# First layer norm's rows made by ScalarE instead of GpSimd, in a new cyclic order of four engines

## The chip, the core and the metric

The kernel runs on one core of one Trainium2 chip. A core has four compute engines that run their own instruction streams: TensorE (PE, matmuls and transposes), VectorE (DVE), ScalarE (ACT) and GpSimd (POOL). SyncE (SP) issues DMAs. They meet only through semaphores. The metric is the device time of the whole program in microseconds; lower is better.

## The reference

Two layers over x of 64 sequences, 128 tokens, 256 features. The phase that matters here is the first layer's attention and its router:

```python
x = x + _L0_xattn_ref(_layernorm(x), ctx_768, mask, Wq, Wk, Wv, Wo)   # 16 heads of 16, softmax over 128 keys
x = x + _L0_ffn_ref(_layernorm(x), w_switch, b_switch, w1, b1, w2, b2) # 8 experts, capacity 512
x = x + _L1_xattn_ref(_layernorm(x), ctx_768, ...)
x = x + _L1_ffn_ref(_layernorm(x), ew, act_w, We, be, Wq, Wk, Wv, Wo, ln_g, ln_b)

def _layernorm(x, axis=-1, eps=1e-05):
    m = jnp.mean(x, axis=axis, keepdims=True)
    v = jnp.var(x, axis=axis, keepdims=True)
    return (x - m) / jnp.sqrt(v + eps)
```

The router picks an expert for each token and counts, over all tokens before it, how many went to the same expert; that count is the token's slot.

## The kernel before, in words

The program has three phases: the first layer's attention with routing (`phase_first_layer`, to about 650 us), the experts (`phase_experts`), and the second layer (`phase_second_layer`), which takes most of the time. The change is in the first.

The phase handles 64 sequences in 32 jobs of two. The steps of a job have short names, and each engine walks through its own list of (step, job) pairs:

- `st` (VectorE): `bn_stats` and `bn_aggr` of the job's x, into mean and variance; `rs` (GpSimd): 1/sqrt(variance + eps), two small operations; `nm`: the normalized rows `xn`, made by GpSimd with a `tensor_scalar` for each sequence (subtract mean, multiply by rstd).
- `Tx`, `K`, `Q`, `V` (TensorE): transpose of `xn`, and the projections. A name with `^` is the VectorE step that empties the product's PSUM bank, such as `Tx^` into `xT`, `Q^`, `K^` (two operations, even and odd heads), `V^`.
- `S0`, `S1` (TensorE): the scores of sequence 0 or 1 for 16 heads in four PSUM banks, one for each strip of four heads. A bf16 mask row is written first (L645), then the products (L654). `S0.x2` (VectorE) is the row maximum of strip 2 (L488), `S0.e2` (ScalarE) its exponentials, four activations with row sums (L432), `S0.i2` (VectorE) the reciprocals of the sums (L491), `S0.n2` (GpSimd) the product that normalizes the probabilities (L384).
- `T0.0`, `T0.1`, `T1.0`, `T1.1` (TensorE): transposes of the probabilities of two strips each (L664), copied out of PSUM by ScalarE (`T0^0` and so on, L438).
- `A`, `O` (TensorE) with `A^`, `O^`: attention output, output projection; `O^` adds x. `st1`, `rs1`, `nm1`: the second layer norm, on VectorE and GpSimd, into a ring `xn1`. `Tn`, `L`: its transpose and the router's logits.
- `r.sh`, `r.ex`, `r.oh`, `r.n`, `r.n^`: the routing of a group of jobs (groups end at jobs 3, 7, ..., 27, 29, 31). `r.oh` (VectorE, L560 to L569) is a chain of 16 small operations that wait for each other. `put` (GpSimd): two indirect DMAs a job that scatter `xn1` into the experts' buffer.

All products but the scores share four PSUM banks in the order in which TensorE writes them: a product waits until the one four before it has been emptied.

The order is cyclic and written out. In `FIRST_PE_ORDER` the entry `A:3` says that in round k the step `A` of job k - 3 runs. `unfold` turns a table into the whole list; `FIRST_PE_TAIL` and `FIRST_DVE_TAIL` put the last jobs' steps at the end in an order of their own, together with the first six fused weights (`F`, `B`) of the second layer. An engine stands still at a step whose inputs are missing, with everything behind it.

SyncE's list: load of x for job j (waits for `nm1` of job j - 4, whose slot in a ring of four it takes), load of the context, store of x1 and of xn1 of job j - 3, and so on.

Of the kernel before, what the change touches and what calls it, by code (L numbers as in the profile page):

```python
# [11 lines left out]
ALU = mybir.AluOpType  # L12
# [4 lines left out]
PAIR = 2  # L17
# [101 lines left out]


FIRST_PE_ORDER = """
K:1 T0.1:3 S1:2 Tx:1 A:3 r.n:6 Q:1 O:3 T1.0:2 T0.0:2 S0:1 V:1 L:5 Tn:4 T1.1:2
"""

FIRST_DVE_ORDER = """
r.oh:5 S0.i0:1 K^:0 S0.i1:1 S1.x0:1 Tx^:0 S1.x1:1 S1.x3:1 S1.i0:1 A^:2 r.n^:5 S1.x2:1 S1.i1:1 Q^:0 S1.i3:1
O^:2 S0.i3:1 S1.i2:1 st1:2 S0.i2:1 S0.x0:0 S0.x1:0 S0.x3:0 V^:0 L^:4 r.sh:4 mk:-1 st:-1 S0.x2:0 Tn^:3
"""

FIRST_ACT_ORDER = """  # L130
S1.e1:1 S1.e3:1 S1.e2:1 T1^0:1 T1^1:1 T0^0:1 T0^1:1 S0.e0:0 S0.e1:0 S0.e3:0 r.ex:4 T1^2:1 S0.e2:0 T1^3:1
T0^3:1 T0^2:1 S1.e0:0
"""

FIRST_POOL_ORDER = """
rs:1 nm:1 rs1:4 S0.n0:2 nm1:4 S0.n1:2 S1.n0:2 S1.n1:2 S1.n3:2 S1.n2:2 S0.n3:2 S0.n2:2 put:9
"""


# [13 lines left out]
def phase_first_layer(nc, io, scratch, keep, cst, consts_in, cell, first):  # L153
# [7 lines left out]
    CAP = int(CAP_FACTOR * B * T / E)  # L161
    JOBS = B // PAIR
    W2 = PAIR * T
    X_RING, ROW_RING, GROUP = 4, 6, 4
    MASK_JOBS, SENDS, RING = 4, 3, 3
    plan = cell_plan()
    fused = fused_weights(plan)
# [52 lines left out]
    with ExitStack() as es:  # L220
# [3 lines left out]
        def sem(name):  # L224
# [8 lines left out]
        one_row = sb("one_row", [P], BF16)  # L233
        stats, mv = sb("stats", [2, PAIR, 6]), sb("mean_var", [2, 2, PAIR, 2])
        veps, rstd = sb("var_eps", [2, 2, PAIR]), sb("rstd", [2, 2, PAIR])
        qT = sb("qT", [2, 2, W2])
        kE, kO = first["kT_even"], sb("kT_odd", [2, 2, W2])
        va = sb("v_even_odd", [2, PAIR, PAIRS_OF_HEADS, 4, 16])
# [31 lines left out]
        stat, var_made, veps_made, rstd_made = \  # L270
            ([sem(f"{n}{i}") for i in range(2)] for n in ("stats_made", "var_made", "veps_made", "rstd_made"))
        zero_made, buf_zeroed = sem("zero_made"), sem("buf_zeroed")
        step, shifted, exped, hot, slots_made = \
            sem("vector_step"), sem("shifted"), sem("exped"), sem("one_hot"), sem("slots_made")

# [83 lines left out]
        def _(pool):  # L359
# [18 lines left out]
            for n, j in on_pool:  # L378
# [6 lines left out]
                                            ALU.mult).then_inc(norm_made, 1)  # L385
                elif n == "rs":
                    rsqrt(0, j)
                elif n == "rs1":
                    rsqrt(1, j)
                elif n == "nm":  # L390
                    if j >= 1:
                        pool.wait_ge(prod, n_prod["Tx", j - 1])
                    normal(xt[:, j % X_RING], xn, 0, j, xn_made)
                elif n == "nm1":
                    if j >= ROW_RING:
                        p = j - ROW_RING
# [21 lines left out]
        def _(act):  # L418
# [7 lines left out]
            for n, j in on_act:  # L426
                if is_round(n):

                    b, r = head_strip(n)
                    act.wait_ge(max_made, n_max[f"S{b}.x{r}", j])  # L430
                    for k in range(4):
                        a = nc.scalar.activation(pr[:, j % 2, b, r, k], S[r][:, k], ACT.Exp, bias=nmax[:, j % 2, b, r, k:k + 1],  # L432
                                                 accum_out=rsum[:, j % 2, b, r, k:k + 1])
                    a.then_inc(exp_made, 1)
                elif is_turn(n):

                    act.wait_ge(turned, n_turn[n, j])
                    nc.scalar.copy(pT[:, int(n[1]), int(n[-1])], bank(n, j)[:]).then_inc(pT_made, 1)  # L438
                elif n == "r.ex":
                    act.wait_ge(shifted, group_at[j] + 1)  # L440
                    t0, t1 = tiles_of[group_at[j]]
                    nc.scalar.activation(e[:, 0:t1 - t0], pb[:, 0:t1 - t0], ACT.Exp).then_inc(exped, 1)
                else:
                    raise ValueError(n)

        @block.vector
        def _(dve):
# [8 lines left out]
            def statistics(src, i, j):  # L456
# [6 lines left out]
                    dve.wait_ge((xn_made, xn1_made)[i], j - 1)  # L463
                for b in range(PAIR):
                    k = V.bn_aggr(mv[:, i, j % 2, b], stats[:, i, b])
                k.then_inc(var_made[i], 1)

            def chain(i):
# [1170 lines left out]
```

## Time and profile before

| | us |
|---|---|
| median of three runs (4090.85 to 4096.52) | 4091.06 |
| the profiled execution's own time | 4089.82 |
| its span | 4088.0 |
| TensorE busy | 4001.1 (98%) |
| ScalarE busy | 2622.6 (64%) |
| VectorE busy | 2392.3 (59%) |
| GpSimd busy | 1930.2 (47%) |

```profile
## 2 busy tenths in 40 slices
PE   8999999999999999999999999999999999999997
PEld 6888886668888888888888888888888888888886
DVE  5777772025566656666666666666665666666553
ACT  6888881215666666666666666666666666666664
POOL 5888883113444444444444444444444444444443
PEclk9999999999999999999999999999999999999999
```

A slice is 102 us, a digit tenths of it. The first phase is the first six slices: there four engines are at seven to nine tenths at once. Busy time on TensorE includes time in which a matmul waits in its pipeline, so it is not a bound by itself. PEclk is the granted clock as a share of 2.4 GHz.

### The profile page before, as it was taken

How to read it: one execution, taken by the hardware profiler on the slowest of the kernel's cores; microseconds unless marked ns; L12 is line 12 of the kernel's file. 1: busy time of each engine (PE TensorE's matmuls, PEld its weight loads, DVE VectorE, ACT ScalarE, POOL GpSimd, SP SyncE). 2: the span in 40 equal slices, each digit the busy share in tenths (PEclk: the TensorE clock that was granted, in tenths of full speed). 3: DMA queues.
4: the chain of work that ended last, by engine and by line, in shares of the span. 5: the costliest groups of instructions: out<-in, count | busy, mean ns of one | idle time of the engine just before them, and what ended most of it. 6: DMA issues, size and time to landing. Idle time of an engine off the chain costs nothing.

```text
span 4088.0 us, 100757 instructions
## 1 busy us (share of the span) xinstructions
PE 4001.1 (98%) x38276; PEld 3410.6 (83%) x38276; DVE 2392.3 (59%) x6184; ACT 2622.6 (64%) x11786; POOL 1930.2 (47%) x2011
## 2 busy tenths in 40 slices
PE   8999999999999999999999999999999999999997
PEld 6888886668888888888888888888888888888886
DVE  5777772025566656666666666666665666666553
ACT  6888881215666666666666666666666666666664
POOL 5888883113444444444444444444444444444443
PEclk9999999999999999999999999999999999999999
DMA  3232214521000000000000000000000000000000
GB/s 104 70 97 70 67 53 138 181 73 35 14 13 16 15 14 14 13 14 17 14 13 13 14 13 13 20 12 12 12 12 12 12 12 12 12 12 12 7 4 9
DMA packets 117866, 129.73 MB, mean 32 GB/s; under 512 B 12006, under 2 KB 110676, under 8 KB 117264
## 3 DMA queue, kind: packets, MB, share of 16 engines
q1 hardware_dynamic: 105648, 109.80, 8.4%
q0 software_dynamic: 6144, 8.43, 0.7%
q8 instruction: 311, 5.10, 0.5%
q10 hardware_dynamic: 5600, 5.07, 0.4%
q14 instruction: 163, 1.34, 0.1%
HBM read 89.68 MB, written 41.94 MB: 32 GB/s over the span
## 4 chain that ended last, share of the span: by engine, by line
PE 76%; DVE 1%; ACT 0%; issue 0%; POOL 0%; POOLq 0%; ACTq 0%
PE c_product L1411 37%; PE c_product L1422 15%; PE c_product L1470 11%; PE c_scores L1460 7%; PE c_product L1493 5%; PE c_product L1481 2%; DVE c_qT L1266 1%; PE c_product L1399 1%; ACT c_probs L1223 0%; PE c_product L1530 0%; ACT c_front_probs L1223 0%; DVE c_nodes L1266 0%; DVE c_neg_max L1275 0%; POOL c_probs L1177 0%; DVE c_nodes L1337 0%
## 5 line engine op out<-in xcount | busy, mean ns | idle before, releaser
L1177 POOL TENSOR_TENSOR c_probs<-c_probs,c_row_inv 128x512 f32<-128x512 f32 x768 | 794.9, 1043 | 1390.4 <-DVE c_row_inv L1278 1384.4
L1223 ACT ACTIVATE c_probs<-c_scores,c_neg_max 128x128 f32<-128x128 f32 x3072 | 1084.3, 407 | 354.0 <-DVE c_neg_max L1275 353.9
L1411 PE MATMUL c_product<-c_nodes,cell_w 128*128 128x256 f32 x4352 | 1067.4, 384 | 4.8 <-DVE c_nodes L1266 3.1
L1411 PEld LDWEIGHTS c_product<-c_nodes,cell_w 128*128 128x128 f32 x4352 | 797.4, 190 | 123.7 <-DVE c_nodes L1266 11.8
L1223 ACT ACTIVATION_READ_ACCUMULATOR c_probs<-c_scores,c_neg_max 128x1 f32 x3072 | 759.3, 247 | 0.0
L1275 DVE TENSOR_REDUCE c_neg_max<-c_scores 128x4 f32<-128x512 f32 x1024 | 658.3, 679 | 169.5 <-PE c_scores L1460 161.7
L1229 ACT COPY c_probsT<-c_product 128x512 f32<-128x512 f32 x768 | 419.8, 600 | 462.2 <-PE c_product L1470 458.2
L1223 ACT ACTIVATE c_front_probs<-c_scores,c_neg_max 128x128 f32<-128x128 f32 x1024 | 364.7, 394 | 170.2 <-DVE c_neg_max L1275 170.2
L1422 PE MATMUL c_product<-cell_w,c_nodes 128*128 128x256 f32 x1792 | 430.3, 381 | 0.0
L432 ACT ACTIVATE a_probs<-a_scores,a_neg_max 128x128 f32<-128x128 f32 x1024 | 361.2, 399 | 83.9 <-DVE a_neg_max L488 83.2
L1470 PE MATMUL c_product<-consts_sb,c_probs 128*128 128x128 f32 x3072 | 404.1, 275 | 5.4 <-POOL c_probs L1177 5.4
L1470 PEld LDWEIGHTS c_product<-consts_sb,c_probs 128*128 128x128 f32 x3072 | 355.4, 141 | 46.6 <-POOL c_probs L1177 7.3
L1177 POOL TENSOR_TENSOR c_front_probs<-c_front_probs,c_row_inv 128x512 f32<-128x512 f32 x256 | 270.0, 1056 | 258.4 <-DVE c_row_inv L1278 256.8
L1422 PEld LDWEIGHTS c_product<-cell_w,c_nodes 128*128 128x128 f32 x1792 | 329.4, 191 | 38.6 <-issue 0.6
L1278 DVE RECIPROCAL c_row_inv<-c_row_sum 128x4 f32<-128x4 f32 x1024 | 167.9, 169 | 329.2 <-ACT c_probs L1223 225.4
L1411 PE MATMUL c_product<-c_oT,cell_w 128*128 128x256 f32 x1280 | 329.3, 380 | 0.0
L384 POOL TENSOR_TENSOR a_probs<-a_probs,a_row_inv 128x512 f32<-128x512 f32 x256 | 258.9, 1041 | 28.6 <-DVE a_row_inv L491 28.5
L1411 PEld LDWEIGHTS c_product<-c_oT,cell_w 128*128 128x128 f32 x1280 | 243.1, 190 | 34.5 <-DVE c_oT L1266 2.3
L1266 DVE TENSOR_SCALAR c_oT<-c_product,cell_b 128x256 f32<-128x256 f32 x384 | 167.8, 478 | 140.0 <-PE c_product L1493 139.1
L1266 DVE TENSOR_SCALAR c_qT<-c_product,cell_b 128x256 f32<-128x256 f32 x384 | 166.3, 474 | 136.4 <-PE c_product L1411 134.8
L432 ACT ACTIVATION_READ_ACCUMULATOR a_probs<-a_scores,a_neg_max 128x1 f32 x1024 | 245.1, 239 | 0.0
L1223 ACT ACTIVATION_READ_ACCUMULATOR c_front_probs<-c_scores,c_neg_max 128x1 f32 x1024 | 238.8, 233 | 0.0
(167 smaller groups left out, 6450.2 us busy)
## 6 DMA issues: line engine op xcount, KB each, us to landing
e_w<-in_L_ffn_w SPq DMA_DIRECT2D x12, 1024.0 KB, 6.2
a_x<-in_x SPq DMA_DIRECT2D x32, 256.0 KB, 2.9
a_ctxT<-in_ctx_pairsT SPq DMA_DIRECT2D x32, 256.0 KB, 3.1
x<-a_x SPq DMA_DIRECT2D x32, 256.0 KB, 2.1
xn<-a_xn SPq DMA_DIRECT2D x32, 256.0 KB, 2.2
c_routed<-xn SPq DMA_DIRECT2D x32, 256.0 KB, 2.7
c_x<-x SPq DMA_DIRECT2D x32, 256.0 KB, 3.1
c_ctxT<-in_ctx_pairsT SPq DMA_DIRECT2D x32, 256.0 KB, 2.8
```

The costliest lines, as they stand in the source:

```text
L384: nc.gpsimd.tensor_tensor(p, p, rinv[:, j % 2, b, r].unsqueeze(2).broadcast_to([P, 4, T]), ALU.mult).then_inc(norm_made, 1)
L432: a = nc.scalar.activation(pr[:, j % 2, b, r, k], S[r][:, k], ACT.Exp, bias=nmax[:, j % 2, b, r, k:k + 1], accum_out=rsum[:, j % 2, b, r, ...
L1177: nc.gpsimd.tensor_tensor(e, e, rinv[:, i, r].unsqueeze(2).broadcast_to([P, 4, T]), ALU.mult).then_inc(norm_made, 1)
L1223: a = nc.scalar.activation(probs(n)[:, r, k], S[r][:, k], ACT.Exp, bias=nmax[:, i, r, k:k + 1], accum_out=rsum[:, i, r, k:k + 1])
L1229: nc.scalar.copy(probsT(n)[:, int(n[-1])], bank(n, j)[:]).then_inc(pT_made, 1)
L1266: k = V.tensor_scalar(dst[:, u], m[:, u], bias[:, u:u + 1], scalar, ALU.add, *([then] if then else []))
L1275: V.tensor_reduce(nmax[:, i, r], S[r][:], AX.X, ALU.max, negate=True).then_inc(max_made, 1)
L1411: i = T_.matmul(m[:, u], w[:, k, u * P:(u + 1) * P], src[:, k], start=n == 0, stop=n == last)
L1422: i = T_.matmul(m[:, b], src[:, k, b * T:(b + 1) * T], w[:, k], start=n == 0, stop=n == len(steps) - 1)
L1460: i = T_.matmul(S[r][:, k], q[e, u, b * T:(b + 1) * T], w[e, u, b * T:(b + 1) * T], start=True, stop=True)
L1470: i = T_.transpose(m[:, k], probs(name)[:, r, k], ident)
L1493: i = T_.matmul(m[32 * r:32 * r + 32, u, b * T:(b + 1) * T], va[:, group(c), b, h:h + 32], pT[:, group(c), r, k], start=True, stop=True)
```

## The change

The normalized rows of the first layer norm are made by ScalarE, as Identity(rstd * x + shift) with shift = -mean * rstd. VectorE writes the negated mean in `st`, GpSimd multiplies it by rstd in `rs`. The four cyclic tables are replaced; the ring of `xn1` grows from 6 to 8 jobs. The tail tables stay.

```diff
 FIRST_PE_ORDER = """
-K:1 T0.1:3 S1:2 Tx:1 A:3 r.n:6 Q:1 O:3 T1.0:2 T0.0:2 S0:1 V:1 L:5 Tn:4 T1.1:2
+Tn:6 Q:1 T0.1:3 T1.1:3 S0:1 A:3 r.n:7 K:0 O:3 T1.0:2 T0.0:2 S1:1 L:6 Tx:0 V:1
 """
 
 FIRST_DVE_ORDER = """
-r.oh:5 S0.i0:1 K^:0 S0.i1:1 S1.x0:1 Tx^:0 S1.x1:1 S1.x3:1 S1.i0:1 A^:2 r.n^:5 S1.x2:1 S1.i1:1 Q^:0 S1.i3:1
-O^:2 S0.i3:1 S1.i2:1 st1:2 S0.i2:1 S0.x0:0 S0.x1:0 S0.x3:0 V^:0 L^:4 r.sh:4 mk:-1 st:-1 S0.x2:0 Tn^:3
+O^:3 S1.i3:2 st1:3 S0.i1:1 S0.i3:1 S0.i0:1 S0.i2:1 S1.x3:1 S1.x2:1 S1.x1:1 Tx^:0 L^:6 S1.x0:1 r.sh:6 V^:1
+Tn^:5 Q^:0 r.oh:6 S1.i1:1 S1.i0:1 st:-1 S0.x2:0 S0.x0:0 S0.x3:0 A^:2 r.n^:6 S1.i2:1 S0.x1:0 mk:-2 K^:-1
 """
 
 FIRST_ACT_ORDER = """
-S1.e1:1 S1.e3:1 S1.e2:1 T1^0:1 T1^1:1 T0^0:1 T0^1:1 S0.e0:0 S0.e1:0 S0.e3:0 r.ex:4 T1^2:1 S0.e2:0 T1^3:1
-T0^3:1 T0^2:1 S1.e0:0
+nm:-1 T0^1:1 S1.e3:0 S1.e2:0 S1.e1:0 r.ex:5 S1.e0:0 T0^3:1 T0^2:1 T1^3:1 T1^2:1 S0.e2:-1 S0.e3:-1 S0.e0:-1
+S0.e1:-1 T1^0:0 T1^1:0 T0^0:0
 """
 
 FIRST_POOL_ORDER = """
-rs:1 nm:1 rs1:4 S0.n0:2 nm1:4 S0.n1:2 S1.n0:2 S1.n1:2 S1.n3:2 S1.n2:2 S0.n3:2 S0.n2:2 put:9
+S0.n3:2 nm1:4 put:11 S0.n1:2 S1.n0:2 rs:0 S0.n2:2 S1.n1:2 S0.n0:2 S1.n2:2 S1.n3:2 rs1:3
 """
...
-    X_RING, ROW_RING, GROUP = 4, 6, 4
+    X_RING, ROW_RING, GROUP = 4, 8, 4
...
                 elif n == "rs":
                     rsqrt(0, j)
+                    pool.wait_ge(rstd_made[0], j + 1)
+                    nc.gpsimd.tensor_tensor(shift[:, j % 2], neg_mean[:, j % 2], rstd[:, 0, j % 2], ALU.mult).then_inc(shift_made, 1)
                 elif n == "rs1":
                     rsqrt(1, j)
-                elif n == "nm":
-                    if j >= 1:
-                        pool.wait_ge(prod, n_prod["Tx", j - 1])
-                    normal(xt[:, j % X_RING], xn, 0, j, xn_made)
...
+                elif n == "nm":
+
+                    act.wait_ge(shift_made, j + 1)
+                    if j >= 1:
+                        act.wait_ge(prod, n_prod["Tx", j - 1])
+                    for b in range(PAIR):
+                        k = nc.scalar.activation(xn[:, b], xt[:, j % X_RING, b], ACT.Identity, bias=shift[:, j % 2, b:b + 1],
+                                                 scale=rstd[:, 0, j % 2, b:b + 1])
+                    k.then_inc(xn_made, 1)
...
                 for b in range(PAIR):
                     k = V.bn_aggr(mv[:, i, j % 2, b], stats[:, i, b])
+                if i == 0:
+                    k.then_inc(mean_made, 1)
+                    dve.wait_ge(mean_made, j + 1)
+                    k = V.tensor_scalar(neg_mean[:, j % 2], mv[:, 0, j % 2, :, 0], -1.0, None, ALU.mult)
                 k.then_inc(var_made[i], 1)
```

## Rows read from the trace of the kernel before

**Rows 1.** Timeline of VectorE: `Tx^`; columns start us, duration us, instruction.

```profile
438.45 0.69 DVE L500 COPY a_xT<-a_product 128x512 f32<-128x512 f32 x1
...
459.30 0.68 DVE L500 COPY a_xT<-a_product 128x512 f32<-128x512 f32 x1
...
478.30 0.69 DVE L500 COPY a_xT<-a_product 128x512 f32<-128x512 f32 x1
...
496.09 0.69 DVE L500 COPY a_xT<-a_product 128x512 f32<-128x512 f32 x1
```

**Rows 2.** Timeline of VectorE: first maxima of `S1`, jobs 1 and 31.

```profile
50.34 0.69 DVE L488 TENSOR_REDUCE a_neg_max<-a_scores 128x4 f32<-128x512 f32 x1 [2.19 <-PE a_scores L654]
...
607.20 1.89 DVE L488 TENSOR_REDUCE a_neg_max<-a_scores 128x4 f32<-128x512 f32 x3
```

**Rows 3.** Groups by line, GpSimd, 263.5 to 281.3 us: count, busy us, mean ns, idle.

```profile
L384 POOL TENSOR_TENSOR a_probs<-a_probs,a_row_inv 128x512 f32<-128x512 f32 x8 | 8.1, 1041 | 0.0
L370 POOL TENSOR_SCALAR a_xn<-a_x,a_mean_var,a_rstd 128x256 f32<-128x256 f32 x4 | 4.9, 1220 | 0.2 <-POOL a_rstd L365 0.2
L411 POOL DMA_INDIRECT buf<-a_xn,slots x2 | 2.1, 1041 | 0.5 <-issue 0.5
L365 POOL TENSOR_TENSOR a_rstd<-a_var_eps,consts_sb 128x2 f32<-128x2 f32 x2 | 1.4, 716 | 0.2
L363 POOL TENSOR_TENSOR a_var_eps<-a_mean_var,consts_sb 128x2 f32<-128x2 f32 x2 | 0.4, 186 | 0.3 <-DVE a_mean_var L465 0.3
```

**Rows 4.** Timeline of TensorE: transposes of probabilities, and mask rows of scores.

```profile
218.77 0.60 PE L664 MATMUL a_product<-consts_sb,a_probs 128*128 128x128 f32 x4
219.59 1.53 PE L664 MATMUL a_product<-consts_sb,a_probs 128*128 128x128 f32 x12 [0.22 <-POOL a_probs L384]
221.05 0.40 PE L645 MATMUL a_scores<-a_mask_add,a_one_row 32*128 32x512 bf16 x4
...
241.30 1.91 PE L664 MATMUL a_product<-consts_sb,a_probs 128*128 128x128 f32 x16
243.14 0.40 PE L645 MATMUL a_scores<-a_mask_add,a_one_row 32*128 32x512 bf16 x4
...
251.04 0.76 PE L645 MATMUL a_scores<-a_mask_add,a_one_row 32*128 32x512 bf16 x4
```

**Rows 5.** Busy us of each engine in stretches of 20 us, then clock, DMA, GB/s.

```profile
220.00:240.00 20.00, 17.32 (x209) 14.86 (x208) 16.52 (x56) 13.89 (x65) 15.36 (x18) 0.91 0.49 154
...
480.00:500.00 20.00, 19.78 (x234) 17.09 (x227) 14.75 (x40) 17.67 (x87) 18.91 (x21) 1.00 0.20 61
```

**Rows 6.** Timelines of TensorE and VectorE in one routing round.

```profile
233.76 3.60 PE L675 MATMUL a_product<-a_probsT,a_v_even_odd 128*32 128x128 f32 x64 [1.78 <-DVE a_kT_odd L506]
...
228.62 0.21 DVE L560 TENSOR_REDUCE a_mx<-a_exp 128x8 f32<-128x64 f32 x1
...
232.33 0.72 DVE L505 TENSOR_SCALAR front_keys<-a_product,consts_sb 128x512 f32<-128x512 f32 x1
```

**Rows 7.** Groups by line and shape, ScalarE, whole program.

```profile
L432 ACT ACTIVATE a_probs<-a_scores,a_neg_max 128x128 f32<-128x128 f32 x1024 | 361.2, 399 | 83.9 <-DVE a_neg_max L488 83.2
...
L438 ACT COPY a_probsT<-a_product 128x512 f32<-128x512 f32 x256 | 141.1, 635 | 15.7 <-PE a_product L664 15.5
...
L432 ACT ACT_TABLE_LOAD x1 | 1.3, 1283 | 24.0 <-DVE a_neg_max L488 24.0
```

**Rows 8.** SyncE's timeline at a load of x, and the loads' median to landing.

```profile
575.13 0.40 SPq L298 DMA_DIRECT2D a_x<-in_x  x1
...
a_x<-in_x SPq DMA_DIRECT2D x28, 256.0 KB, 2.8
```

**Rows 9.** Timelines of GpSimd and TensorE at the phase's end.

```profile
629.16 2.43 POOL L370 TENSOR_SCALAR a_xn<-a_x,a_mean_var,a_rstd 128x256 f32<-128x256 f32 x2 [0.21 <-POOL a_rstd L365]
...
646.57 0.97 POOL L411 DMA_INDIRECT buf<-a_xn,slots  x1 [0.30 <-issue]
...
653.16 1.57 PE L831 MATMUL e_turned<-consts_sb,front_keys 128*128 128x128 f32 x8 [1.35 <-DMA front_keys<-buf]
```

More of the change, by code:

```diff
@@ L235, in phase_first_layer @@
         veps, rstd = sb("var_eps", [2, 2, PAIR]), sb("rstd", [2, 2, PAIR])
+        neg_mean, shift = sb("neg_mean", [2, PAIR]), sb("shift", [2, PAIR])
         qT = sb("qT", [2, 2, W2])
@@ L272, in phase_first_layer @@
         zero_made, buf_zeroed = sem("zero_made"), sem("buf_zeroed")
+        mean_made, shift_made = sem("mean_made"), sem("shift_made")
         step, shifted, exped, hot, slots_made = \
```

## The prediction

> **What bounds the kernel now.** The table of engines comes first: TensorE is busy for 98% of the span, and the change touches only the first of three phases, which ends with the first expert matmul near 653 us. A busy TensorE looks like a bound, so the second view is the beat of the phase. The copy `Tx^` runs once a job: its starts stand 17.79 us apart in plain jobs, and 20.85 and 19.00 us apart in the two around a routing group [rows 1]. Between the score maxima of job 1 and those of job 31 lie 556.86 us [rows 2]; 30 beats of 17.79 are 533.7, so the routing groups, of which seven fall in or at the edge of this stretch, cost 23.2 us, 3.3 each.
>
> Third, GpSimd over one beat (17.8 us): 8.1 for the probabilities' products, 4.9 for both layer norms, 2.1 for the indirect DMAs, 1.4 and 0.4 for the small steps and 0.9 of gaps, together 17.8 [rows 3]. It never rests: GpSimd sets the plain beat, and TensorE's busy share hides that. Fourth, what TensorE loses in such a beat. Sixteen transposes take 1.84 us from start to start where nothing is waited for (241.30 to 243.14), and 2.28 where the last twelve wait for GpSimd's product (218.77 to 221.05); the mask rows of a round of scores take 0.40 us unhindered (243.14), and 0.76 where they wait for exponentials (251.04) [rows 4]. Without these two losses of 0.44 and 0.36 the beat would be 16.99 us: TensorE's floor.
>
> Fifth, the routing stall. `r.oh` holds VectorE from 228.62 to 232.25, `K^` comes only behind it at 232.33, and the matmuls of `A`, which need the bank that `K^` empties, start after 1.78 us of idling and last 3.60 us instead of 1.9, because the granted clock has fallen from 2.4 to 1.2 GHz (mean 0.91 in this stretch) [rows 5, 6].
>
> **The change, part by part.**
> Taken off GpSimd: two TENSOR_SCALAR of 1.22 us a job [rows 3], 2.4 us. Added: one product of 2 columns, nearest to L363's 0.19 us [rows 3], and a wait for rstd of about 0.2. GpSimd then needs 17.8 - 2.4 + 0.4 = 15.8 us with its waits. It stops being the bound.
>
> Added on ScalarE: two Identity activations of 256 columns with scale and bias. None is in the trace. Below: two Exp of 128 columns, 0.40 us each; above: two copies of 512 columns, 0.64 us each [rows 7]. So 0.8 to 1.3 us for the pair; 1.0 taken, between both. In a plain stretch ScalarE is busy for 17.67 of 20 us [rows 5], 15.7 of a beat; with the pair 16.7, which is 0.3 under TensorE's floor. At the upper bound it is the floor itself.
> The Trainium skill, ScalarE: Activation LUTs, section What ACT_TABLE_LOAD costs, speaks against this price: an ACTIVATE with one pointer operand takes 280 ns and 0.833 ns a column, a second pointer adds 93 ns. An estimate by it is 1.08 us for the pair, and a ScalarE sum of 16.8 us; the forecast would not move. No row here shows that form.
>
> Added on VectorE: a 2-column negation after the aggregates, 0.17 us like the reciprocals, and a wait of some 0.1 us for its own result. VectorE is busy for 14.75 of 20 us [rows 5], 13.1 of a beat; 13.4 does not bind.
>
> **The new order.** It adds no matmul. I laid its cycle out with TensorE at its floor (time 0 is the start of `Tn:6`; `S0` starts at 4.1, `A` 5.4, `K` 7.3, `O` 9.0, `T1.0` 10.7, `S1` 12.6, `Tx` 14.6, `V` 15.1) and looked for links that come too late. `A` needs the four pT copies of ScalarE just in time; `O` needs `A^` with 1 us to spare; the bank of `T0.0` needs `K^` with 1.1; that of the second `T0.0` strip needs `O^` with 0.65; `Tx` needs ScalarE's `nm` with 0.5, and `nm` needs GpSimd's shift with 6. `S0` and `S1` find their score banks emptied 1 us before. The tightest ring runs through the load of x: `nm1` ends, SyncE issues the store and then the load (0.4 us an issue), it lands 2.8 us later [rows 8], and `st` must follow before VectorE's `S0.x2`; about 0.8 us is left. All fit at 16.99, with half a microsecond in several places, so I take **17.2** as the beat: 16.99 and 0.2 for waits that the layout leaves out.
>
> In the routing round `r.oh` now stands ahead of `S0.x2`, `A^` and `K^`, and it still costs 3.6 us. `A^` comes 1.0 us too late for `O`, `K^` 0.5 more for `T0.0`, `O^` 0.2 more, and r.n's own matmuls are 0.5: 2.2 us instead of 3.3. Idle pieces of 1.0 and 0.5 us instead of 1.78 should mostly spare the fall of the clock. Bounds: 0.5 (its work alone) and 4.3 (the 3.06 and 1.21 of [rows 1]).
>
> The sum: 30 x 17.2 + 6 x 2.2 = 529.2 against 556.86, **-27.7 us** (the seventh group falls in the drain).
>
> **Fill.** `S1` of job 0 now needs no full round of its own: `S0`, `K`, `S1` stand in one round. The table load (1.28 us [rows 7]) moves ahead of the first `nm`, where it delays the first transposes by 0.3 us, and leaves the first Exp. By my layout job 1's maxima come 3 us earlier (bounds -5 and +1).
>
> **Drain.** Here the deeper order takes back. Before, `nm1` of the last job ends at 631.59, 24.4 us after the landmark at 607.20; then six `put` follow, 12 indirect DMAs to 647.54, so 2.54 us a `put` without the one wait of 0.7; the experts start at 653.16 [rows 2, 9]. After, `put:11` leaves eight of them behind that `nm1` (20.3 us), and `nm1` itself ends some 26.7 us after the landmark, because `S1.n3` and `O` of the last job come later. 26.7 + 20.3 + 5.6 = 52.6 instead of 46.0: **+6.6 us**. TensorE has run out of fused-weight work by then and may start the experts at 1.2 GHz: +1.
>
> Total -27.7 - 3 + 6.6 + 1 = -23.1 us. The profiled execution took 4089.82 us, 1.2 below the median of the three runs, so 4066.7 for it and **4068 us** on the median's footing. What stands behind the first phase runs the same instructions.
>
> **Rivals.**
> *The ring through x holds the beat* (16%). `st` now has about 0.8 us to spare, where before nothing waited for x. Loads that land 1 us later in traffic with the scatters would push `st`, the shift, six products, `nm1` and so the next load. If the beat stayed at 17.79: 533.7 + 13.2 = 546.9, -10; with the fill and the drain -5.4, **4086**. For it: GpSimd's chain is in the ring. Against it: the sum of the ring's links is about 15.8 us.
>
> *The table swings back and forth* (8%, the slower side). Should Identity and Exp not share a table, ScalarE would load twice a job: 16.7 + 2 x 1.28 = 19.3 us [rows 7]. It decides once ScalarE's sum passes 17.2. 30 x 19.3 + 13.2 = 592.2, +35.3; with the fill and drain +39.9, **4131 us**. Against it: the whole program has one load of 1.28 us [rows 7], though Exp, Copy and Relu alternate in it; for it: Identity is not in the trace. The Trainium skill, ScalarE: Activation LUTs, section Table sets, says that cheap functions, identity among them, are in every set; the trace's one load agrees as far as it goes.
>
> *Better than laid out* (12%). The beat comes to 17.0, the routing round costs its work and little else (1.0), and TensorE's leftover hides half of the drain: 30 x 17.0 + 6 = 516, -41, -3 +4: **4051**.
>
> *The forecast* (64%): beat 17.0 to 17.4, routing 1.5 to 3.3, drain +4 to +9: 4056 to 4082.
>
> **How the numbers follow.** A measurement of this kernel can tell about 0.2%, 8 us, from no change. Faster than 4083: the forecast, the better case and a quarter of the ring's rival, 0.80. Same: the rest of that rival, 0.12. Slower: the table, 0.08. The range 4050 to 4086 leaves out the table, half of the better case and the ring's upper part.
>
> **What would show it.** Right: `Tx^` starts 17.0 to 17.4 us apart in plain jobs; GpSimd waits for VectorE some 2 us a beat; no wait of 1.78 us before `A`, but one of about 1 us before `O` on `A^` in each fourth job; job 31's maxima near 574 us; eight `put` after the last `nm1`, and the experts at about 627 to 632 us. The Identity pair at 0.8 to 1.1 us from start to end. Wrong: `bn_stats` waiting for the x DMA with the score maxima behind it (the ring); more than one ACT_TABLE_LOAD; a beat set by a new wait of TensorE for ScalarE's copies, which have the least room of all; or a clock that falls in each routing round again, 1.2 us each.

## The result

The change makes the kernel 0.16% faster, where 0.56% was forecast: 4084.05 us median against 4089.82 for the kernel before on the same chips (14 runs each), a ratio of 0.9984 with the 95% interval 0.9976 to 0.9992. That is the "same" case, not the forecast one. The profiled execution has a span of 4079.6 us.

First the beat of the first phase, the starts of `Tx^` on VectorE (start us, duration us, instruction), and at the first maxima of `S1` in jobs 1 and 31, the landmarks of [rows 2]:

```profile
438.38 0.68 DVE L513 COPY a_xT<-a_product 128x512 f32<-128x512 f32 x1
455.22 0.68 DVE L513 COPY a_xT<-a_product 128x512 f32<-128x512 f32 x1
475.81 0.68 DVE L513 COPY a_xT<-a_product 128x512 f32<-128x512 f32 x1
492.65 0.68 DVE L513 COPY a_xT<-a_product 128x512 f32<-128x512 f32 x1
...
48.88 1.29 DVE L501 TENSOR_REDUCE a_neg_max<-a_scores 128x4 f32<-128x512 f32 x2 [1.05 <-PE a_scores L667]
...
578.14 1.89 DVE L501 TENSOR_REDUCE a_neg_max<-a_scores 128x4 f32<-128x512 f32 x3 [1.05 <-PE a_scores L667]
```

A plain job takes 16.84 us in these rows (before 17.79, [rows 1]), a routing job 20.59. Between the landmarks lie 529.26 us; before, they lay 556.86 apart. So the body of the phase gained 27.6 us, as forecast. Busy time in stretches of 20 us (columns as in [rows 5]) shows TensorE without a pause in these two, at 2.4 GHz:

```profile
220.00:240.00 20.00, 20.00 (x271) 17.91 (x270) 15.31 (x45) 19.32 (x83) 17.62 (x22) 1.00 0.24 82
480.00:500.00 20.00, 20.00 (x301) 17.91 (x303) 16.03 (x45) 18.65 (x82) 18.17 (x22) 1.00 0.28 94
```

The rest is at the end of the phase. TensorE's, GpSimd's and VectorE's timelines behind the landmark at 578.14 (in brackets: idle time before, and what ended it), then the busy time of the whole stretch:

```profile
598.22 0.66 PE L723 MATMUL a_product<-a_one_hot,consts_sb 128*128 128x64 f32 x2 [3.04 <-DVE a_tokens_before L582]
601.80 3.02 PE L688 MATMUL a_product<-a_probsT,a_v_even_odd 128*32 128x128 f32 x64
635.63 3.75 PE L637 MATMUL a_product<-a_edge_w,a_edgeT 128*128 128x256 f32 x8 [4.07 <-DVE cell_w L540]
644.29 1.29 PE L738 MATMUL a_product<-be,a_edge_w 128*128 128x1 f32 x8
646.17 1.06 PE L844 MATMUL e_turned<-consts_sb,front_keys 128*128 128x128 f32 x8 [0.59 <-PEq L220]
...
609.63 0.20 POOL L365 TENSOR_TENSOR a_var_eps<-a_mean_var,consts_sb 128x2 f32<-128x2 f32 x1 [10.56 <-DVE a_mean_var L474]
610.84 2.43 POOL L372 TENSOR_SCALAR a_xn<-a_x,a_mean_var,a_rstd 128x256 f32<-128x256 f32 x2 [0.20 <-POOL a_rstd L367]
633.09 0.97 POOL L411 DMA_INDIRECT buf<-a_xn,slots  x1 [0.30 <-issue]
...
634.73 0.75 DVE L540 TENSOR_SCALAR cell_w<-a_product,ew 128x512 f32<-128x512 f32 x1 [5.02 <-remote]
...
578.14:646.17 68.03, 54.27 (x376) 48.05 (x377) 30.76 (x111) 12.93 (x48) 36.90 (x38) 0.77 0.18 54
```

From the landmark to the first expert matmul it takes 68.03 us, where it took 45.96 before [rows 2, 9]. Of the 27.6 us won in the body and 1.5 in the fill (48.88 against 50.34), 22.1 are given back here, and the experts start only 7.0 us sooner (646.17 against 653.16). Behind them the program takes 3433.4 us against 3434.8. These rows show four things that the experiments below take up: TensorE waits 3.04 us for the one-hot additions of the last full group, with `A` of job 31 queued behind it; its clock is low (mean 0.77, before 0.90); it waits 4.07 us for a copy that VectorE starts only at 634.73, after 5.02 us in which it did nothing; and `B5`, its own leftover work, ends at 645.6, just ahead of the experts.

The price of the moved rows, by line and on the timeline of ScalarE in a plain round:

```profile
L445 ACT ACTIVATE a_xn<-a_x,a_shift,a_rstd 128x256 f32<-128x256 f32 x64 | 38.1, 697 | 0.0
L445 ACT ACT_TABLE_LOAD x1 | 1.3, 1283 | 13.2 <-POOL a_shift L391 13.2
...
275.38 1.22 ACT L445 ACTIVATE a_xn<-a_x,a_shift,a_rstd 128x256 f32<-128x256 f32 x2
```

The two activations overlap. From the start of the first to the end of the second it is 1.22 us; ScalarE's next step starts 1.0 us after the first one's start.

### The profile page after: what moved, and what is told of

Read it like the earlier page. It is cut to its first block, busy times and chain, and to the rows that moved or that the text cites. A ratio compares the mean times of both kernels' runs of the same rounds, so it can differ in the third digit from the quotient of the medians.

```text
span 4079.6 us, 100819 instructions
## 1 busy us (share of the span) xinstructions
PE 3987.1 (98%) x38276; PEld 3404.4 (83%) x38276; DVE 2399.0 (59%) x6216; ACT 2645.8 (65%) x11850; POOL 1863.0 (46%) x1979
## 4 chain that ended last, share of the span: by engine, by line
PE 76%; DVE 1%; ACT 0%; issue 0%; POOL 0%; POOLq 0%; ACTq 0%
PE c_product L1424 37%; PE c_product L1435 15%; PE c_product L1483 10%; PE c_scores L1473 7%; PE c_product L1506 5%; PE c_product L1494 2%; DVE c_qT L1279 1%; PE c_product L1412 1%; ACT c_probs L1236 0%; PE c_product L1543 0%; ACT c_front_probs L1236 0%; DVE c_nodes L1279 0%; DVE c_neg_max L1288 0%; POOL c_probs L1190 0%; DVE c_nodes L1350 0%
## 5 line engine op out<-in xcount | busy, mean ns | idle before, releaser
L432 ACT ACTIVATION_READ_ACCUMULATOR a_probs<-a_scores,a_neg_max 128x1 f32 x1024 | 257.7, 255 | 0.0
L1279 DVE TENSOR_SCALAR c_kT<-c_product,cell_b 128x256 f32<-128x256 f32 x384 | 167.1, 477 | 122.5 <-PE c_product L1424 122.4
```

The costliest lines, as they stand in the source:

```text
L1279: k = V.tensor_scalar(dst[:, u], m[:, u], bias[:, u:u + 1], scalar, ALU.add, *([then] if then else []))
```

## The experiments

Every kernel ran beside the kernel before on the same chip. "Drain" is the time from the landmark of job 31 to the first expert matmul, "body" that between the landmarks; both, and the start of the experts, come from one profiled execution of each kernel. The last six kernels of the table ran once each.

| Kernel | median us | ratio to before (95%) | body | drain | experts start |
|---|---|---|---|---|---|
| before | 4089.82 | | 556.86 | 45.96 | 653.16 |
| after | 4084.05 | 0.9984 (0.9976 to 0.9992) | 529.26 | 68.03 | 646.17 |
| e1, after again | 4083.43 | 0.9985 (0.9976 to 0.9994) | 532.18 | 66.44 | 646.75 |
| e2, puts early | 4084.45 | 0.9985 (0.9976 to 0.9994) | 530.10 | 72.51 | 652.13 |
| e3, A early | 4078.84 | 0.9973 (0.9964 to 0.9982) | 530.60 | 64.30 | 642.93 |
| e4, both | 4081.39 | 0.9968 (0.9956 to 0.9979) | 531.61 | 63.62 | 644.32 |
| e5, F early | 4080.94 | 0.9980 (0.9971 to 0.9989) | 528.90 | 65.82 | 644.00 |
| e6, old order | 4096.62 | 1.0016 (1.0007 to 1.0025) | 557.68 | 47.7 | 653.5 |
| e7, rows on GpSimd | 4105.58 | 1.0042 (1.0028 to 1.0056) | 552.21 | 71.2 | 676.1 |
| e9, last job first | 4074.83 | 0.9966 (0.9954 to 0.9978) | 529.43 | 58.14 | 635.53 |
| e11, A^ ahead | 4151.29 | 1.0153 (1.0139 to 1.0167) | 611.05 | 57.0 | 716.1 |
| e12, slots late | 4066.82 | 0.9938 (0.9925 to 0.9952) | 525.59 | 56.52 | 630.68 |
| e8, e3 without late puts | 4081.09 | | 529.93 | 62.33 | 641.63 |
| e15, e8 again | 4076.50 | | 528.37 | 60.27 | 637.16 |
| e13, e9 again | 4076.01 | | 530.30 | 58.39 | 637.00 |
| e10, e9 without late puts | 4078.74 | | 533.64 | 55.96 | 637.75 |
| e16, e10 again | 4059.30 | | 529.65 | 47.71 | 626.05 |
| e14, e12 again | 4071.30 | | 526.04 | 58.48 | 632.48 |

What stands behind the experts' start runs the same instructions in all kernels, yet it took between 3433 and 3445 us (an execution's time less its start of the experts). So a few us between two medians need not come from the phase. Two profiled executions are far from their kernel's median: that of e7 (4120.68) is the slowest of five, that of e6 (4089.86) the fastest of eleven.

**What the two halves of the change do alone.** e6 keeps the rows on ScalarE and takes back the old orders:

```diff
-nm:-1 T0^1:1 S1.e3:0 S1.e2:0 S1.e1:0 r.ex:5 S1.e0:0 ...
+... r.ex:4 T1^2:1 S0.e2:0 T1^3:1
+nm:-1 T0^3:1 T0^2:1 S1.e0:0
```
(the orders and tails of TensorE, VectorE and GpSimd are those of before, without GpSimd's `nm`).

> One part alone: the rows of the first layer norm on ScalarE, with the cyclic orders and tails of the kernel before (nm stands between T1^3 and T0^3 on ScalarE; the rings are those of after). Theory A (the order makes the shorter round, the move only allows it): the plain round stays within 0.3 us of the 17.79 us of before, since GpSimd's 2.4 us of rows lay beside a TensorE that was busy; the median is within 3 us of before. Rival B (the move makes the gain): the round falls by about 0.9 us, as in after, and the drain stays at 46 us, so that the median is some 20 us under before.

e7 keeps the new orders and puts the rows back on GpSimd (the steps `nm` on ScalarE, the shift and the negated mean are gone):

```diff
-S0.n3:2 nm1:4 put:11 S0.n1:2 S1.n0:2 rs:0 S0.n2:2 ...
+S0.n3:2 nm1:4 put:11 S0.n1:2 S1.n0:2 rs:0 nm:0 S0.n2:2 ...
```

> The other part alone: the new orders and tails with the rows back on GpSimd (behind rs of the same job). Theory A (GpSimd has 17.2 of 20 us busy in after, so 2.4 us more nearly fill it, and what it normalizes comes late): the plain round is 17.8 to 19.5 us, the body 30 to 70 us longer than in after. Rival B (GpSimd has room enough): the round stays at 16.84 us, and the median is that of after within 3 us.

`Tx^` in e6, then in e7, then what TensorE waits for between 200 and 560 us in e7, in after and in e6 (total us, times, longest):

```profile
420.20 0.69 DVE L513 COPY a_xT<-a_product 128x512 f32<-128x512 f32 x1 [0.20 <-PE a_product L630]
438.17 0.69 DVE L513 COPY a_xT<-a_product 128x512 f32<-128x512 f32 x1 [0.19 <-PE a_product L630]
```

```profile
457.68 0.68 DVE L511 COPY a_xT<-a_product 128x512 f32<-128x512 f32 x1
475.26 0.68 DVE L511 COPY a_xT<-a_product 128x512 f32<-128x512 f32 x1
...
PE a_product L675 <- POOL a_probs L386: 16.6, 32, 1.1
```

```profile
PE a_product L677 <- DVE a_kT_odd L519: 6.9, 5, 1.4
PE a_product L644 <- DVE a_oT L526: 5.4, 5, 1.2
```

```profile
PE a_product L688 <- DVE a_kT_odd L519: 9.3, 5, 1.9
```

In e6 the plain round is 17.97 us, no shorter than before: theory A for the round. Its median is 8.6 us over that of before on the same chip (4087.98), not within 3, and the profiled execution, as fast as before, doesn't show why. GpSimd is relieved (280.00 us busy between 200 and 560 us, before 320.10) and now waits 52.5 us there for VectorE's reciprocals (before 13.2), but the round doesn't shrink: other links of the old order are as tight. Which ones is not shown. In e7 a plain round takes 17.42 to 19.07 us from the third job on, and TensorE waits 32 times for GpSimd's products between 200 and 560 us, which it never does in after. That is theory A in kind; its size was put too high (the body is 23 us longer than in after, not 30 to 70). Neither half is worth anything alone, and both are slower than before; the 27.6 us need the relieved GpSimd and the order together.

**Repeat.** e1 is after unchanged.

> The changed kernel once more, unchanged, to see which of its waits at the end of the first phase belong to it and which to one execution. In the first trace the last norm's nm1 ended 35.1 us after the first score maxima of job 31 (before: 24.4), and VectorE then stood still for 5.0 us (629.70 to 634.73) until an instruction fetch at 634.28 had ended. Theory A (the order of the last jobs' steps is what takes the gain back): the 35.1 us and TensorE's wait of about 3 us ahead of the count matmuls of job 27 (r.n) return exactly; ratio to before 0.9975 to 0.9992. Theory B (the late fetch is a property of this program's code layout): the stall of 5 us returns too, at the same instruction. If it were chance: it is gone and the experts start about 4 us sooner.

Drain 66.4 us, ratio 0.9985: the long drain belongs to the kernel, theory A. The wait of 3.04 us for the one-hot additions is there again, and `nm1` of job 31 ends 36.7 us behind the landmark (35.1 in after). The stall of 5 us did not return at its instruction, against theory B; others of 3.90 and 2.64 us stand at the two steps before it that empty a product. The instruction fetch that theory B rests on is not at 634.28 us: in after the trace has one from 623.2 to 623.7 us and none from there to the experts' start.

**Where the drain's time goes.** e2 starts the last scatters in GpSimd's idle time:

```diff
+FIRST_POOL_TAIL = """
+put:8 put:7 put:6 put:5 rs1:1 nm1:1 put:4 put:3 put:2 put:1
+"""
```

> Only GpSimd's last steps are reordered: put of jobs 24 to 27 stands ahead of rs1 and nm1 of job 31, in the 10.6 us in which GpSimd waited for that job's statistics. Theory A': the chain of scatters behind the last nm1 is a link of its own: four of them (10.2 us) move into the gap, the last scatter ends near 624 instead of 634 (it must still wait for the slots of jobs 30 and 31, which were made at 629.0), so the gain is bounded by these slots: last scatter near 631 to 633, experts 2 to 3 us sooner, ratio to before 0.9975. Rival: TensorE's fused-weight work, which ended at 645.6, sets the start of the experts, and the ratio stays at that of the repeated kernel within 1 us.

The scatters did fill the gap, but the experts came no sooner. The median is that of e1 (4084.45 and 4083.43), and in the profiled execution the drain is 4.5 us longer than in after: the products of `A` of job 31 had been started at 604.85, but VectorE got to copy them only at 615.41, and `O` followed.

```profile
615.41 0.69 DVE L531 COPY a_oT<-a_product 128x512 f32<-128x512 f32 x1 [9.77 <-remote]
```

"Remote" is a wait for which the profile shows no releaser; TensorE's last record of these products runs from 609.47 to 609.91. No instruction fetch lies between 604 and 631 us.

e3 moves `A` of job 31 ahead of the routing of group 27 on TensorE and VectorE:

```diff
-A:1 O:1 L:3 Tn:2 F0:1 L:2 ...
+A:1 r.n:5 O:1 L:4 Tn:3 L:3 Tn:2 F0:1 L:2 ...
-A^:1 O^:1 st1:1 L^:3 r.sh:3 Tn^:2 ...
+A^:1 r.n^:5 O^:1 L^:4 st1:1 Tn^:3 L^:3 r.sh:3 Tn^:2 ...
```

> Only the tail tables of TensorE and VectorE are changed: A of job 31 stands ahead of r.n of job 27, and O of job 31 ahead of L of job 28 and Tn of job 29. Theory A: TensorE no longer waits 3.0 us for the counts before the last A; A of job 31 starts about 596.7 instead of 601.8 and at full clock, nm1 of job 31 ends 28 us after the landmark instead of 35, and the experts start 6 to 8 us sooner; ratio to before 0.9965. Rival (the drain is bounded from the other side, by the scatters' slots, the fetch of instructions and TensorE's work at low clock): nm1 moves, the experts' start does not, less than 2 us.

e4 is e3 with one put ahead of `nm1` of job 31 (`put:8 rs1:1 nm1:1 put:7 ...`).

> Both edits together, with put of job 24 ahead of the last rs1 and the rest behind nm1. Theory A: the drain from the landmark to the first expert transposes falls from 68 us to 52 to 55, near the 52.6 that the prediction had for the changed kernel, and the whole to 4068 to 4073 us: ratio to before 0.995 to 0.9965. If this comes, the error of the prediction is the drain alone and its cause is the order in which the tail is walked. Rival: the sum of the other two, or less, because TensorE's own work and the fetch are next.

The end of `nm1` of job 31 and the start of the experts in e3:

```profile
607.48 2.43 POOL L372 TENSOR_SCALAR a_xn<-a_x,a_mean_var,a_rstd 128x256 f32<-128x256 f32 x2 [0.21 <-POOL a_rstd L367]
...
642.93 1.07 PE L844 MATMUL e_turned<-consts_sb,front_keys 128*128 128x128 f32 x8 [0.59 <-PEq L220]
```

So `nm1` ends 31.3 us behind the landmark (578.63) instead of 35.1, and the drain is 3.7 us shorter than in after, 2.1 than in e1; the median falls by 4.6 against e1. The wait for the routing was real, though at most a sixth of the 22.1 us given back, and less than the 6 to 8 us of theory A. e4 adds nothing that can be told from e3; its drain is 63.6 us and not the 52 to 55 of its theory. In e3 VectorE waited 3.88 us for a logit product, the last 2.4 of them after its end, and TensorE's own work ended at 642.35, 0.6 ahead of the experts.

e5 fills TensorE's waits with the fused-weight products (the diff is against e3):

```diff
-A:1 r.n:5 O:1 L:4 Tn:3 L:3 Tn:2 F0:1 L:2 Tn:1 r.n:3 B0:1 L:1 F1:1 ...
+A:1 r.n:5 F0:1 O:1 L:4 Tn:3 F1:1 B0:1 L:3 Tn:2 B1:1 F2:1 L:2 Tn:1 B2:1 r.n:3 F3:1 L:1 B3:1 F4:1 r.n:1 ...
```

> The tails of e3_a31_early, with the fused-weight products moved forward: F0 ahead of O of job 31, F1 and B0 behind Tn of job 29, B1 and F2 behind Tn of job 30, B2 behind Tn of job 31, the rest as before. Nothing is left out. Theory A (the experts' start is set by TensorE's own leftover work, run at half clock because its waits let the clock fall): the products fill waits of 0.7 to 2.1 us, the clock stays at 1.0 for longer, TensorE's last B ends 5 to 8 us sooner than the 642.35 us of e3 against the landmark 578.63 (63.7 us behind it), and the experts start at about landmark + 58 us, held then by the last put; the median is 4 to 6 us under e3 (about 4074). Rival B (the experts' start is set by the last put and the load of rows): start and median stay within 1 us of e3.

Half right. TensorE was through at 638.5, 5.5 us before the experts, so its leftover no longer set their start, yet the drain was 65.8 us, and the ratio is no better than that of e3. In its place stands a chain through the last job's routing (VectorE, TensorE, GpSimd, TensorE):

```profile
626.27 0.17 DVE L550 TENSOR_TENSOR a_logits<-a_product,a_b_switch 128x16 f32<-128x16 f32 x1 [2.88 <-issue]
...
631.18 0.61 PE L724 MATMUL a_product<-a_one_hot,consts_sb 128*128 128x32 f32 x2 [7.07 <-DVE a_tokens_before L583]
...
637.44 0.97 POOL L412 DMA_INDIRECT buf<-a_xn,slots  x1 [0.31 <-issue]
...
644.00 1.94 PE L845 MATMUL e_turned<-consts_sb,front_keys 128*128 128x128 f32 x8 [5.51 <-PEq L221]
```

The logits of job 31 were made by 621.4 and copied only at 626.27, 4.9 us later; the last scatter ended at 638.4, and the experts came 5.6 us behind it. Both bounds stand a few us apart, and taking away one leaves the other.

e8 and its repeat e15 are e3 without the last 16 indirect DMAs (the rows of the last eight jobs don't reach the experts):

```diff
                 elif n == "put":
+                    if j >= JOBS - 8:
+                        continue
```

> e3_a31_early with the scatters of jobs 24 to 31 left out (16 indirect DMAs; the rows of those jobs don't reach the experts' buffer, and so the output isn't the reference's). Theory A (the late releases of VectorE behind TensorE's products in the drain, 3.88 us before L of job 31, come from the burst of indirect DMAs): they are gone, no wait of VectorE for 'remote' over 0.5 us; the experts start no sooner than TensorE's own last product, about landmark + 60 us. Rival B (they come from something else, as instruction fetches): they stay at 2 to 4 us. Rival C (puts set the experts' start): the start moves to under landmark + 55 us.

> e8_no_late_puts unchanged (e3 without the scatters of jobs 24 to 31), a second execution. If the burst of indirect DMAs is what delays the releases, there is none over 1 us here either. One over 2 us would acquit the burst.

Once the remaining indirect DMAs are over, no release is late in either: VectorE's longest wait there, 2.7 us in e8 and 2.2 in e15, ends with the product that it is put down to. One of 1.45 us stands in both just before, at `A^` of job 31, beside the last two indirect DMAs that are left (its rows are in the last section). The drain is 62.33 and 60.27 us, 2 to 4 us less than e3's, and the experts start 0.6 us behind TensorE's own work: theory A, with that work as the next bound.

**A better end.** e9 combines these: F0 to F2 fill the waits, and `L` of job 31 with its routing goes ahead of `F3`.

```diff
+A:1 r.n:5 F0:1 O:1 L:4 Tn:3 F1:1 B0:1 L:3 Tn:2 B1:1 F2:1 L:2 Tn:1 r.n:3 B2:1 L:1 F3:1 B3:1 r.n:1 F4:1 B4:1 F5:1 B5:1
```
(VectorE's copies in the same order, its `r.oh:1` ahead of `F3^:1`).

> New tails on top of those of e4_both_tails (one put ahead of nm1 of job 31): F0 to F2 and B0, B1 fill TensorE's waits as in e5, and L of job 31 comes right behind Tn of job 31, its routing ahead of F3. Nothing is left out. Theory (in e5 the last puts set the experts' start, since L of job 31 stood behind F3 and its copy came 4.9 us after the product, in the burst of indirect DMAs; TensorE had ended 5.5 us before): L of job 31 is copied at about landmark + 39 us instead of + 48.1, the last put ends by landmark + 54, and the experts start at landmark + 57 to + 60 (e5: 65.8, e3: 64.3); the median is 6 to 8 us under e5, about 4074. Rival (the late releases come whatever stands there): the start stays at + 63 or more, the median within 3 us of e5.

> e9_last_first unchanged, a second execution under the profile. If the late releases (a wait of VectorE of 2 us and more for a product that TensorE had ended, put down to remote or issue; in e9 4.1 us before L of job 31) belong to the order of this kernel, they are at the same place with the same size, and the experts start at landmark + 58 again. If they are chance, they are elsewhere or gone, and the start then is at landmark + 53 to + 58.

The late copy of job 31's logits and the start of the experts in e9:

```profile
619.09 0.17 DVE L555 TENSOR_TENSOR a_logits<-a_product,a_b_switch 128x16 f32<-128x16 f32 x1 [4.13 <-PE a_product L744]
...
635.53 1.94 PE L850 MATMUL e_turned<-consts_sb,front_keys 128*128 128x128 f32 x8 [2.53 <-PEq L226]
```

The drain is 58.14 us in e9 and 58.39 in e13: 8 to 10 us less than in after and e1, as the theory had it. The late release came in both at this place, with waits of 4.13 and 2.72 us; in both the copy starts 4.6 us behind the product's last record. The experts start 5.6 us behind the last scatter: the scatters set their start.

e10 and e16 are e9 without the last 16 indirect DMAs, as in e8.

> e9_last_first with the scatters of jobs 24 to 31 left out (16 indirect DMAs; those rows don't reach the experts' buffer). If the late releases come from the burst, no wait of VectorE is put down to 'remote' or 'issue' for over 1 us, as in e8, and the experts start at TensorE's last product, landmark + 50 to + 54 us. If TensorE's clock alone made e8's length, the start is at + 54 or less with a mean clock over 0.9 between landmark and start. If neither holds, the start stays at + 60.

> e10_last_first_no_puts unchanged (e9 without the scatters of jobs 24 to 31), a second execution. If the burst is the cause, no release is late by over 1 us. For the clock: it falls to 0.5 again in a stretch in which TensorE is busy without a pause, if the work there (products of 1, 8 and 32 columns beside those of 256) is what lowers it; if e10's fall was chance, the mean from landmark to start is over 0.9.

Their drains are 56.0 and 47.71 us, though the kernel is the same. Busy time in stretches (columns as in [rows 5]), first e10, then e16:

```profile
610.00:620.00 10.00, 10.00 (x53) 9.40 (x52) 6.25 (x28) 0.23 (x1) 1.82 (x2) 0.63 0.36 105
620.00:630.00 10.00, 10.00 (x34) 8.78 (x34) 5.37 (x26) 0.23 (x1) 0.00 (x0) 0.50 0.52 158
```

```profile
610.00:620.00 10.00, 10.00 (x57) 9.00 (x55) 7.23 (x34) 0.23 (x1) 0.00 (x0) 0.71 0.59 179
620.00:630.00 10.00, 8.46 (x48) 6.80 (x48) 4.89 (x15) 0.00 (x0) 0.00 (x0) 1.00 0.34 84
```

TensorE is busy without a pause from 610 us to its last product in both (625.46 in e16), and in e10 it stays at 1.2 GHz through the second stretch; in e16 it is at 2.4. `nm1` of job 31 ends 30.0 us behind the landmark in both; the drains differ by 8.3 us, and the clock is what the rows show to differ (mean 0.79 and 0.93 over the drain). It can be low while TensorE is busy without a pause. That goes against half of e5's theory: filling the waits is not enough to hold the clock.

**The routing round.** In a routing round of after TensorE waits 1.18 us for `A^` before `O`, and 1.38 for `K^` before the last transposes; with the 0.6 of the routing's own matmuls that is most of the 3.75 us. e11 moves `A^` ahead of the maxima, and two groups of reciprocals ahead of `r.oh` (the rest is e9):

```diff
-Tn^:5 Q^:0 r.oh:6 S1.i1:1 S1.i0:1 st:-1 S0.x2:0 S0.x0:0 S0.x3:0 A^:2 r.n^:6
+Tn^:5 Q^:0 S1.i1:1 S1.i0:1 r.oh:6 st:-1 A^:2 S0.x2:0 S0.x0:0 S0.x3:0 r.n^:6
```

> e9_last_first with one change in VectorE's cyclic order: the reciprocals S1.i1 and S1.i0 ahead of r.oh, and the copy A^ ahead of the maxima S0.x2, S0.x0, S0.x3. Nothing is left out. Theory (a routing job costs 3.75 us because A^ and K^ come 1.2 and 1.4 us late behind r.oh and what is queued after it): the wait of O for A^ in a routing round (1.17 us) goes, the routing round is longer than a plain one by 2.3 to 3.0 us instead of 3.75, seven times, 5 to 10 us in all; plain rounds stay at 16.84. Rival (A^ ahead of the maxima waits for TensorE in plain rounds): each plain round gets longer by up to 0.6 us, and the body by up to 15 us.

The rival, and far worse than it said: 18.98 us a plain round, and 4151 us. The plain round in e11 (VectorE, ScalarE):

```profile
340.05 0.69 DVE L532 COPY a_oT<-a_product 128x512 f32<-128x512 f32 x1 [2.09 <-PE a_product L694]
340.66 1.88 DVE L507 TENSOR_REDUCE a_neg_max<-a_scores 128x4 f32<-128x512 f32 x3
...
341.37 0.37 ACT L438 ACTIVATE a_probs<-a_scores,a_neg_max 128x128 f32<-128x128 f32 x1 [2.83 <-DVE a_neg_max L507]
```

And the same wait of ScalarE in after:

```profile
268.47 0.37 ACT L432 ACTIVATE a_probs<-a_scores,a_neg_max 128x128 f32<-128x128 f32 x1 [0.71 <-DVE a_neg_max L501]
```

VectorE stands 2.09 us before `A`'s products with three maxima behind it whose scores are ready, and ScalarE, which waits 0.71 us at that place in after, now waits 2.83. Its wait grew by 2.12 us and the round by 2.14: less its wait, ScalarE's round is 16.1 us in both. So ScalarE, which next to TensorE has the least room (busy for 328 of the 360 us from 200 to 560 in after), is the bound here by this match of two numbers; no run tests it alone. The routing rounds did not get their gain either: they take 23.4 to 23.9 us.

e12 is e9 with the slots' arithmetic moved behind the keys:

```diff
-... A^:2 r.n^:6 S1.i2:1 S0.x1:0 mk:-2 K^:-1
+... A^:2 S1.i2:1 S0.x1:0 mk:-2 K^:-1 r.n^:6
```

> e9_last_first with one change in VectorE's cyclic order: the routing's last part r.n^ (1.6 to 2.5 us) moved behind the copies K^. Nothing is left out. Theory (TensorE's 1.4 us wait for K^ in a routing round is r.n^ standing ahead of K^ on VectorE): that wait goes, the routing round falls from 20.6 to 19.0 to 19.5 us, plain rounds stay at 16.84, and the body is 7 to 10 us shorter; the median is 6 to 9 us under e9, about 4067. Rival (the late work only moves on: O^, st1 and the copies behind them come 1.4 us late instead): the routing round stays over 20.3 us and the median within 2 us of e9.

> e12_slots_late unchanged, a second execution under the profile. e12 had the same burst of indirect DMAs and no late release. If they are chance, one of 2 to 5 us may show here; if they belong to the order, none does and the start is at landmark + 56.5 again, the last put's end + 5.6 us.

```profile
452.49 0.68 DVE L519 COPY a_xT<-a_product 128x512 f32<-128x512 f32 x1
472.40 0.68 DVE L519 COPY a_xT<-a_product 128x512 f32<-128x512 f32 x1
...
327.28 0.63 PE L683 MATMUL a_product<-consts_sb,a_probs 128*128 128x128 f32 x4 [0.84 <-DVE a_x L534]
```

The routing round is 19.91 us, not 19.0 to 19.5: of the 1.38 us, 0.7 is saved, and TensorE waits 0.84 for `O^` instead. The body is 3.8 us shorter, not 7 to 10. The median fell by 8.0, as the theory said, but the traces show 4.8 us of it (the start of the experts, and the two profiled executions); e12's drain was also shorter, by 1.6. e14, the same kernel, has a late release of 4.09 us where e12 had none, and a drain of 58.48. e12 is the fastest kernel with all its work, 0.62% (0.48 to 0.75%) under before.

## Why the prediction was wrong

**What set the old beat.** The prediction has GpSimd set it, from one round in which GpSimd never rests. Between 200 and 560 us GpSimd waits 24.5 us for VectorE in the kernel before, and in e6 it is relieved and the round stays. So GpSimd was at most one of several bounds; only its relief and the new order together shortened the round.

**The beat.** Forecast 17.2, measured 16.84, under the 16.99 that was taken for TensorE's floor. The 0.2 us for what the layout left out was not needed in most rounds.

**ScalarE's pair.** Taken at 1.0 us, measured 1.0 from the pair's start to the start of what follows, with one table load in the program: the slower rival is out. From start to end it is 1.22 us, over the 0.8 to 1.1 of the sign. The Trainium skill, ScalarE: Activation LUTs, section What ACT_TABLE_LOAD costs, gave an estimate of 1.08 us, between these two. As the text feared, ScalarE has little room: it is busy for 19.3 and 18.7 of 20 us, and e11 shows the price.

**The ring through x.** VectorE's waits before `bn_stats` in after:

```profile
DVE a_stats L468 <- DMA a_x<-in_x: 11.8, 17, 2.0
```

Waits of up to 0.6 us stand mostly in rounds of 16.84 us, so the ring doesn't hold the beat, and the rival is out. But the slack of 0.8 us was about right: the four waits over 1.3 us stand in rounds of 17.01 to 17.85 us. In e1 there are six (1.35 to 2.11 us), in rounds of 17.05 to 17.88, and its body is 2.9 us longer than after's. So the ring seems to hold single rounds; no run takes it away.

**Routing.** Forecast 2.2 us a group, measured 3.75, inside the bounds of 0.5 to 4.3. The late links were the ones named, `A^` before `O` (forecast 1.0, measured 1.18) and `K^` before `T0.0` (forecast 0.5 more, measured 1.38 more). The second is the mis-sized one; e12, with `r.n^` behind `K^`, gets 0.7 us of it back. The clock did not fall again: it is at 1.00 in every stretch of 20 us from 60 to 580 us.

**The body.** Forecast 529.2, measured 529.26, but two misses cancel: 30 x 16.84 = 505.2 and 6 x 3.75 = 22.5 make 527.7, and 1.6 is the balance of the longer rounds just named and shorter ones near the start (16.52). That the sum came out to 0.1 us is luck.

**The fill.** Forecast -3, measured -1.46, within its bounds.

**The drain: the step that failed.** Of the 14.7 us between the 4066.7 that was forecast for the profiled execution and its 4081.36, 14.4 are here. Forecast 52.6 + 1, measured 68.03. By its own terms: `nm1` of the last job ends 35.1 us behind the landmark, not 26.7 (+8.4); the sixteen scatters take 20.8 us, not 20.3 (+0.5); from the last of them to the experts it is 12.1, not 5.6 (+6.5); the sum is 15.4, of which 1 was counted for the clock.
The first term was taken from before with 2.3 us for the later `S1.n3` and `O`. But in the new order `V` of job 31, two small steps and the last sixteen transposes of job 30 still stand between the landmark and `A` of job 30, which in the old order follows at once; 2.54 us of waiting for ScalarE's copies, which stand behind `S1`'s exponentials, and 3.04 us for the one-hot additions come on top. In the body a round lies between that wait and `A`; in the drain the rounds shrink and it does not. e3, with `A` of job 31 ahead of that wait, gives 3.8 us of the 8.4 back.
The third term was right as a price and wrong as a bound: where the scatters set the start, it is 5.6 us again (e5, e9, e12). In after TensorE's leftover set it, which the prediction had called exhausted by then. Of that leftover's delay 4.07 us are TensorE's wait for VectorE's late copy. With the clock at 0.77 TensorE is busy for 54.27 us of the drain, before for 38.97 at 0.90 and with less work (332 matmuls counted against 376): the text counted 1 us for the clock.

So of the 14.4 us missed the order of the tail holds 8 to 10 (after and e1 68.0 and 66.4, e9 and e13 58.1 and 58.4, with all work done). No run splits the rest. The clock and the late releases are the candidates: e16, without the last scatters and at a mean clock of 0.93, has 47.7, and e10, the same kernel at 0.79, 56.0.

## What to carry over

A new cyclic order is won in its rounds and paid at its ends: lay out the drain by hand as carefully as the round, with each engine's leftover work as a bound of its own, at the low clock. A relieved engine and a new order may be worth nothing alone (e6 +0.16%, e7 +0.42%) and something together. In a round that is full, find the engines with the least room and never queue their input behind another engine's wait: in e11 2.12 us more of it came with 2.14 us a round.

## What was unexpected of the hardware

**Late releases beside indirect DMAs.** VectorE waits for a product of TensorE well past its modelled end, without a releaser in the profile or with an older one: in e2 the last record of `A` of job 31 ends at 609.9 and the copy starts at 615.41. Counted from the product's end, VectorE waited for 5.5 us in e2, 6.63 in e7, 5.02 and 2.60 in after, 3.90 and 2.64 in e1, 2.4 in e3, 2.88 in e5, 4.13 in e9, 4.11 in e11, 2.72 in e13, 4.09 in e14, and 1.5 in e4. These came during, or up to 1.7 us behind, a series of indirect DMAs 1.28 us apart, and not in every execution of one kernel (none in e12; e14 is e12's kernel). Nor did the twelve behind the last `nm1` in before and e6 bring one.

In the four executions without the last sixteen (e8, e10, e15, e16) there was none of 2 us. There is one of 1.45 to 1.48 us in each, at `A^` of job 31, beside the last two indirect DMAs that are left; it is also in e3, e9 and others with that tail, but not in e12. TensorE's products, GpSimd's indirect DMA and the copy in e10:

```profile
599.13 2.05 PE L696 MATMUL a_product<-a_probsT,a_v_even_odd 128*32 128x128 f32 x64 [0.29 <-ACT a_probsT L446]
...
601.75 0.99 POOL L419 DMA_INDIRECT buf<-a_xn,slots  x1 [0.30 <-issue]
...
603.24 0.69 DVE L534 COPY a_oT<-a_product 128x512 f32<-128x512 f32 x1 [1.48 <-PE a_product L732]
```

So waits of over 2 us go with a series of eight or more indirect DMAs in every run here; four executions without the last sixteen are few to say that they need it. A late instruction fetch is not the cause in e2, where none lies near the wait. What in the series holds VectorE is open, and no run told it apart.

**The clock of a busy TensorE.** In the body of after the granted clock stays at 2.4 GHz (1.00 in every stretch). In its drain it is at 1.2 GHz from 615 to 625 us (0.50), though TensorE is busy for all of these 10 us. The same holds for e10 from 620 to 630 us, while the same kernel in e16 has 2.4 GHz there. What decides between the two is open.
